# Ten instead of twelve score maxima ahead of the first attention step, and parts 5 and 6 of that step with three each

## The reference, cut to what matters

```python
h = tokens(x)                       # embedding, grouped convolution over 2 tokens, relu: (2, 1024, 128)
h = h + attn(layernorm(h))          # 8 heads of 64, 1024 tokens, batch 2, plus its own input
h = h + ffn(layernorm(h))           # norm, linear, 8 experts (128 -> 512 -> 128), gelu, linear, gelu
# inside attn, for each of 16 (batch, head):
dots = einsum('bhqd,bhkd->bhqk', q, k) * 64 ** -0.5
attn = softmax(dots, axis=-1)       # needs the maximum over all keys of each query
out = einsum('bhqk,bhkd->bhqd', attn, v)
```

## Time and profile before

| | us |
|---|---|
| median of 3 timed executions | 391.29 |
| lowest and highest of them | 390.88, 1285.34 |
| the profiled execution | 390.81 |
| its span, first to last instruction | 388.6 |

### The profile page before, as it was taken

One profiled execution on the slowest core, in us unless ns is written; L12 is line 12 of the kernel. 1 busy time (PEld: TensorE's weight loads), 2 busy tenths in 40 slices (PEclk: granted clock), 3 DMA queues, 4 the chain that ended last, 5 costly groups with the idle time before them and its releaser, 6 DMA issues.

```text
span 388.6 us, 6731 instructions
## 1 busy us (share of the span) xinstructions
PE 380.0 (98%) x2386; PEld 223.3 (57%) x2386; DVE 267.3 (69%) x474; ACT 273.0 (70%) x388; POOL 293.8 (76%) x145
## 2 busy tenths in 40 slices
PE   8999999999999999999999999999999999999996
PEld 8756545554454455544545554464446644589995
DVE  6998677777867786777777776868785545565222
ACT  3566656687968886887788778958882589337753
POOL 3080476969999999999999999999999599700021
PEclk9999999999999999999999999999999999999999
DMA  4001002101222022202211341252025105000001
GB/s 148 6 0 37 17 3 57 55 2 55 58 55 44 14 56 56 55 3 62 49 55 34 64 126 55 57 153 65 5 58 164 55 3 163 0 2 15 14 29 54
DMA packets 28228, 19.45 MB, mean 50 GB/s; under 512 B 21248, under 2 KB 23680, under 8 KB 28196
## 3 DMA queue, kind: packets, MB, share of 16 engines
q1 hardware_dynamic: 27620, 18.05, 17.5%
q10 hardware_dynamic: 576, 0.98, 0.8%
HBM read 17.72 MB, written 1.17 MB: 49 GB/s over the span
## 4 chain that ended last, share of the span: by engine, by line
PE 93%; DVE 4%; issue 1%; ACT 1%; DVEq 0%
PE psum L669 31%; PE psum L658 25%; PE psum L596 11%; PE psum L584 5%; PE psum L605 4%; PE psum L726 4%; PE psum L715 4%; PE psum L560 3%; PE psum L680 2%; PE psum L535 1%; PE psum L621 1%; PE psum L623 1%; PE psum L734 1%; PE psum L509 1%; PE psum L693 1%
## 5 line engine op out<-in xcount | busy, mean ns | idle before, releaser
L1088 DVE TENSOR_REDUCE half_maxes<-psum 128x1 f32<-128x512 f32 x232 | 149.1, 684 | 36.6 <-PE psum L596 35.8
L855 ACT ACTIVATE probs<-psum 128x1024 f32<-128x1024 f32 x128 | 124.5, 1022 | 59.0 <-PE psum L658 58.7
L669 PE MATMUL psum<-probs,v_all 128*64 128x512 f32 x512 | 123.7, 604 | 0.0
L1305 POOL TENSOR_TENSOR sums<-sums,probs 128x1024 f32<-128x1024 f32 x31 | 74.1, 2391 | 3.4 <-ACT probs L855 3.4
L1305 POOL TENSOR_TENSOR odd_sum<-odd_sum,probs 128x1024 f32<-128x1024 f32 x31 | 74.0, 2388 | 0.0
L669 PEld LDWEIGHTS psum<-probs,v_all 128*64 128x64 f32 x512 | 31.2, 136 | 62.5 <-issue 43.2
L1305 POOL TENSOR_TENSOR sums<-probs 128x1024 f32<-128x1024 f32 x16 | 38.0, 2373 | 29.1 <-ACT probs L855 29.1
L596 PE MATMUL psum<-k_round,q_round 64*128 64x512 f32 x256 | 57.0, 446 | 2.0 <-DVE half_maxes L1088 1.1
L1133 DVE TENSOR_SCALAR psum<-max_plane 128x512 f32<-128x512 f32 (+1 forms) x48 | 38.2, 805 | 29.3 <-ACT probs L855 27.9
L596 PEld LDWEIGHTS psum<-k_round,q_round 64*128 64x128 f32 x256 | 24.0, 184 | 54.0 <-DVE half_maxes L1088 41.5
L658 PE MATMUL psum<-q_round,k_round 64*128 64x512 f32 x256 | 52.2, 403 | 0.1
(11 more groups left out here) (123 smaller groups left out, 453.2 us busy)
## 6 DMA issues: line engine op xcount, KB each, us to landing
max_plane<-rows_scratch SPq DMA_DIRECT2D x16, 512.0 KB, 3.7
inv_sb<-inv_scratch SPq DMA_DIRECT2D x14, 256.0 KB, 3.9
max_rows_of<-maxes SPq DMA_DIRECT2D x128, 0.5 KB, 2.0
v_all<-in_fc SPq DMA_DIRECT2D x4, 512.0 KB, 5.8
fc_late<-in_fc SPq DMA_DIRECT2D x4, 512.0 KB, 5.8
out_h<-probs SPq DMA_DIRECT2D x8, 128.0 KB, 1.8
v_all<-in_w ACTq DMA_DIRECT2D x3, 256.0 KB, 3.5
woT<-in_wo SPq DMA_DIRECT2D x1, 256.0 KB, 3.5
```

The costliest lines, as they stand in the source:

```text
L669: last = pe.matmul(out_bank[head_rows(h), :], v_all[:, s, kc, head_rows(h)], probs[unit(s, kc, half) % TILES][:, h, :], start=(kc == 0), s ...
L855: last = act.activation(probs[u % TILES][:, heads, :], source, ACT.Exp, scale=SCALE)
L1088: dve.reduce_max(half_maxes[:, h, qc, keys:keys + 1], slot[:, h, :], AX.X).then_inc(maxed, 1)
L1305: pool.tensor_tensor(chain[:, :, :], first[:, :, :], probs[kc][:, :, :], ALU.add).then_inc(own, 1)
```

## The change

`AHEAD` goes from 12 to 10: M10 and M11 leave the prologue, and the products of v numbered 12 to 15 stand behind M9 instead of M10. The parts 0 to 7 of step 0 hold 1, 2, 3, 3, 3, 3, 3, 2 maxima: M10; M11, M12; M13 to M15; M16 to M18; M19 to M21; M22 to M24; M25 to M27; M28, M29. From M28 on all maxima stand where they stood. Unit (0, 4, 1) is no longer filled and takes its maxima by a fourth pair of matmuls. In parts with three maxima the order is written anew: both shares of DVE come behind the second unit. The ring stands one bank further from part 7 on.

```diff
-AHEAD = 12
+AHEAD = 10
...
 VALUES_BEHIND = {("q", 0): (0, 1), ("max", *MAXES[2]): (2, 3, 4, 5), ("max", *MAXES[5]): (6, 7),
-                 ("max", *MAXES[7]): (8, 9, 10, 11), ("max", *MAXES[10]): (12, 13, 14, 15)}
+                 ("max", *MAXES[7]): (8, 9, 10, 11), ("max", *MAXES[9]): (12, 13, 14, 15)}
...
-FIRST_PLANES = [(0, kc, 0) for kc in (2, 3, 6)] + [(0, kc, 1) for kc in (0, 1, 2, 3)]
+FIRST_PLANES = [(0, kc, 0) for kc in (2, 3, 6)] + [(0, kc, 1) for kc in (0, 1, 2, 3, 4)]
...
-FIRST_COUNTS = (1, 2, 3, 3, 3)
+FIRST_COUNTS = (1, 2, 3, 3, 3, 3, 3)
...
     elif len(maxes) == 3:
-        items = [maxes[0], first] + shares[0] + [maxes[1], second] + shares[1] + maxes[2:]
+        items = [maxes[0], first, maxes[1], second] + shares[0] + shares[1] + maxes[2:]
```

## The result

The changed kernel takes 392.18 us (median of 14; 392.01 to 392.73) against 391.04 us of the kernel before: a ratio of 1.0032, 95% interval 1.0025 to 1.0039. It is slower by 1.0 to 1.5 us, the best estimate 1.25 us, and far inside 2%. The forecast was 393.1 us, 2.1 us slower, with a range that holds the result.

What follows compares the result with a forecast made beforehand. PE (TensorE), busy 380.0 of 388.6 us, was taken to bound the kernel. The terms −0.47 − 0.1 + 0.85 + 0.68 + 1.14 = +2.1 us, from 391.0, gave 393.1 us; range 391.1 to 394.4 us.

Steps and rivals of the forecast that it cites:

- (a): Prologue: M10 and M11 leave, saving two pairs of 0.23 us, while the 0.88 us wait stays: −0.47 us.
- (b): Part 2: M15's join moves behind the third maximum's reductions, so the second and third maximum come earlier: −0.1 us.
- (c): Part 4: the late join makes the rows late, and PE stands 1.0 us for them, partly regained: +0.85 us.
- Rival 1: The rows come in time in part 4, so only parts 5 and 6 cost: +1.25, 392.2 us; chance 0.2.
- (d): Part 5 takes three maxima instead of two, 5.05 instead of 4.37 us: +0.68 us.
- (e): Part 6: three maxima instead of two, and unit (0,4,1)'s fourth pair free: 5.05 instead of 3.91 us, +1.14.
- (f): Part 6: the share of (0,6,1), behind two maxima's reductions, delays only the third's reduction: 0 us.
- (g): From part 7 to the end: old order, ring one bank on, `nt` copied in two instructions: 0 us, bound ±0.3.
- Rival 3: Parts 5 and 6 just stream, so moved pairs cost what they saved: +0.1, 391.1 us; chance 0.15.
- the pace of the ring: Parts with three maxima: DVE's reductions space the maxima 1.37 us apart; part 4 takes 0.45 us more than streaming.

Runs made afterwards that it cites:

- the late join: The changed kernel with two maxima in part 2 and three in parts 3 to 7, so M15's join comes later: 395.24 us, ratio 1.0118.
- the two best versions: The kernel before with maxima 0, 3, 3, 3, 3 in parts 0 to 4, and one or both units of part 5 filled: 390.00 and 389.84 us.

## Why the prediction was right, and where it was wrong

The direction, the place and the range held, and the forecast was 0.9 us too high. By its steps:

- (a), two pairs of 0.23 us saved in the prologue and the 0.88 us of waiting passed on from M12 and M13 to M10 and M11: right, −0.48 us.
- (b), the join out of the way of the second and third maximum: −0.04 for −0.1 us, in the noise of such distances.
- (c), the wait for the rows, is the step that failed, by the size of its term: +0.07 us for +0.85. The mechanism was right (the weight load waits for the row DMAs, and the late join shows 2.4 us of it). The size was the difference of two nearly equal times, and both of its inputs were a little off: the path took 6.47 us instead of the 7.17 that I carried over from the earlier trace rows, and the weight load, to which I gave 0.2 us behind the wait, starts with the matmuls in the record. Against this, the issue came 0.1 us later in part 2 than I had it. Together they turned 1.0 us of standing into 0.2. And the 7.17 us were not the path's fixed length: 0.68 of them fell on one late issue, while code was being loaded. Rival 1, 392.2 us because the DMAs issue faster than before, describes the result but for the last 0.2 us of wait; I gave it 0.2.
- (d) and (e), a third maximum in parts 5 and 6: +0.68 and +1.14 us, right to the hundredth in this trace, since parts of that kind stood in the trace before. That the fourth pair is free there was shown from both sides: 0.23 us in a streaming part, nothing in a part of three.
- (f), no cost of the share where it now stands: right. What it would cost in the old order I put at 0.6 us; it is 1.2, the wait for the exponential and the share itself.
- (g), nothing at the end and nothing absorbed: right within its 0.3 us. From part 7 to the end it is 0.25 us more in the first pair of traces and 0.1 in the second, of 317.
- Rival 3, that parts 5 and 6 would stream: its mark was the distance of the first two maxima, 1.26 us or 1.37. In the changed kernel's part 5 it is 1.38 (63.11 to 64.49).
- The name I gave to the extra 0.45 us, the pace of the ring, covers two things: the waits for a reduction, and a changeover of array layout that takes 0.43 us instead of 0.33 behind a pair that stands alone. For the waits the ring is the cause by the order of the code and by what the records name as their end, and VectorE, busy for 3.87 to 4.55 of some 5.05 us in such parts, is not full; but no run gives the maxima a fourth bank. It didn't matter for this change, where whole parts were exchanged, and it made the experiment with the third maximum between values come out 1.2 us from its expectation.
- That the range held is partly its width, 3.3 us for a change of 1.25; the forecast itself was off by most of the measured change. And 7.8 us is not what a measurement here can tell from nothing: the intervals above are 0.55 to 1.2 us wide.

## What to carry to other kernels

Where an order is written by hand around a small ring of buffers, price a moved item by the whole stage that it joins, read from a stage of that kind in the trace: here an item that costs 0.23 us of work alone cost 0.68 us in its new place, and a fourth pair that costs 0.23 us alone cost nothing. Look first for two users of the ring that stand back to back, since interleaving them with work already there cost nothing here and gave 0.65 us. A wait worked out as the difference of two long paths should be given as a range as wide as the paths vary between like kernels, not as its middle; and before a path's length is carried over, look whether one of its steps was held up by something that need not come again.

## What the runs showed that I had not expected

- Eight DMAs of 0.5 KB, issued back to back on SP, occupied its queue for 5.01 or 5.02 us in nine traces, and for 5.69 and 5.75 us in both profiles of the kernel before, 5.81 us in that kernel with (0,4,1) unfilled, 5.49 and 5.60 us in the two best versions. A 16 KB transfer of code begins 0.1 to 0.3 us behind the first issue in these five and in none of the nine. The Trainium skill says that issuing is usually small relative to the DMA itself (DMA: Bandwidth & Descriptors, section Issuing engines are not separate DMA queues). Here one transfer lands in 2.0 us, and eight issues take at least 4.98, so that the rows can't land 2.4 us behind the first issue, by 54.5 us, as the prediction estimated from that page. The 2.0 us of fixed cost are given there for DMAs issued from GpSimd (section Anatomy of one DMA); these are issued from SP and land in the same time.
- One matmul pair in another tiling mode, set into the middle of eight values, cost 0.58 us, of which 0.35 were for the two changes of mode.
- The opening was 0.48 us longer in the profiled execution of the changed kernel than in that of the kernel before; over all 14 traces M8 comes at 32.67 to 33.33 us. This nearly made up for the term that I had wrong: the span alone, 390.7 us, would have confirmed the wrong sum.
